# Cross-attention block with a routed mixture of experts: another order of the attention's last tiles, waits by bank, and a split of the tail's row sums

## What is computed

```python
x = x + xattn(layernorm(x), ctx, ctx, mask)   # 2 x 1024 rows of 256, 64 keys, 16 heads
x = x + ffn(layernorm(x))
# ffn, xf = the rows after the layer norm:
xa = xf @ P_w.T
C1, C2, C3 = (top3_softmax(xa @ U.T) for U in (U1, U2, U3))   # [rows, 12], three non-zeros a row
h = gelu(sum_e C1[:, e] * (xf @ W1[e].T))
y = sum_e C2[:, e] * (h @ W2[e].T) + C3 @ b2
```

## Time and profile before

| | |
|---|---|
| time, median of 3 runs (lowest to highest) | 380.97 us (378.94 to 382.95) |
| the profiled execution, its own time | 382.12 us |
| its span, first to last instruction | 380.4 us |
| busy, share of the span: PE, DVE, ACT, POOL | 86%, 67%, 52%, 62% |
| mean granted TensorE clock (1.00 is 2.4 GHz, 0.50 is 1.2 GHz) | 0.933 |

### The profile page before, as it was taken

The page is one execution under the profiler, slowest core; times in us unless marked ns, Lnnn a source line. Parts: engine busy times, 40 slices in busy tenths (PEclk is TensorE's granted clock), DMA queues, the critical chain, the costliest instruction groups (busy, mean ns, idle before and its releaser), DMA issues.

```text
span 380.4 us, 7721 instructions
## 1 busy us (share of the span) xinstructions
PE 326.9 (86%) x2071; PEld 287.2 (76%) x2071; DVE 253.9 (67%) x842; ACT 198.6 (52%) x485; POOL 236.5 (62%) x335
## 2 busy tenths in 40 slices
PE   4879989998987668598798979989998979999970
PEld 3569889987977657487788968868887979997850
DVE  3899878897877741646687825576759435553795
ACT  2477989995856604013666751333316756871000
POOL 4359578766875771100677776777724777776692
PEclk9999999998989965879899999989999998999995
DMA  7900111321311282300466736552244766740973
GB/s 221 370 14 4 57 55 57 116 83 57 99 61 44 90 294 70 106 0 15 130 190 206 246 126 223 187 186 105 103 150 130 224 195 188 216 154 1 332 271 117
DMA packets 33889, 52.21 MB, mean 137 GB/s; under 512 B 6090, under 2 KB 23860, under 8 KB 33720
## 3 DMA queue, kind: packets, MB, share of 16 engines
q1 hardware_dynamic: 26472, 35.35, 29.5%
q0 software_dynamic: 6816, 16.24, 11.9%
q10 hardware_dynamic: 560, 0.13, 0.2%
HBM read 29.75 MB, written 24.82 MB: 143 GB/s over the span
## 4 chain that ended last, share of the span: by engine, by line
PE 53%; DVE 15%; issue 10%; POOL 9%; ACT 6%; DMA 4%; DVEq 0%; SPq 0%; ACTq 0%; POOLq 0%
PE banks L1657 32%; PE banks L1940 3%; PE banks L1746 3%; PE banks L1728 3%; PE banks L1703 2%; POOL w_l L592 2%; POOL list_rows L720 2%; PE banks L1713 2%; PE banks L1716 2%; PE banks L1718 2%; DVE q_hl L1070 2%; DMA y_token<-prob,bo_sb 1%; DMA late_rows<-list_rows 1%; PE banks L1789 1%; DVE xn L1279 1%
## 5 line engine op out<-in xcount | busy, mean ns | idle before, releaser
L1657 PE MATMUL banks<-w_h,xd 128*128 128x512 f32 x288 | 96.2, 416 | 2.8 <-ACT prob L931 2.8
L1657 PE MATMUL banks<-w_h,bt 128*128 x328 | 71.0, 309 | 4.8 <-DVE bt L1442 4.8
L1657 PEld LDWEIGHTS banks<-w_h,xd 128*128 128x128 f32 x288 | 56.7, 200 | 16.5 <-issue 3.2
L1657 PE MATMUL banks<-w_l,xd 128*128 128x512 f32 x144 | 59.3, 412 | 0.0
L1657 PEld LDWEIGHTS banks<-w_h,bt 128*128 128x128 f32 x328 | 51.3, 194 | 7.6 <-issue 6.4
L694 POOL DMA_INDIRECT y_token<-prob,bo_sb x42 | 41.0, 975 | 23.4 <-DVE bo_sb L1444 13.3
L1657 PE MATMUL banks<-w_l,bt 128*128 x164 | 47.2, 288 | 0.0
L694 POOL DMA_INDIRECT y_token<-prob_t,bo_sb x40 | 39.6, 989 | 12.1 <-issue 6.0
L1279 DVE SCALAR_TENSOR_TENSOR xf_t<-banks,mask_all,xf_t 128x256 f32<-128x256 f32 x60 | 25.6, 479 | 24.0 <-ACT xf_t L841 12.2
L1442 DVE TENSOR_TENSOR bt<-banks,bt 128x256 fp32r<-128x256 f32 x82 | 33.9, 416 | 9.6 <-ACT bt L925 9.5
L925 ACT ACTIVATE bt<-banks 128x256 fp32r<-128x256 f32 x82 | 30.9, 381 | 15.3 <-PE banks L1940 14.7
(11 more groups left out here) (231 smaller groups left out, 762.7 us busy)
## 6 DMA issues: line engine op xcount, KB each, us to landing
late_rows<-list_rows SPq DMA_DIRECT2D x62, 136.0 KB, 2.8
stage<-in_w_t_dram SPq DMA_DIRECT2D x12, 512.0 KB, 3.7
list_rows<-wo_sb SPq DMA_DIRECT2D x26, 136.0 KB, 2.5
stage<-y_token SPq DMA_DIRECT2D x8, 384.0 KB
late_rows<-y_token SPq DMA_DIRECT2D x6, 384.0 KB, 3.8
mid<-y_token SPq DMA_DIRECT2D x6, 384.0 KB, 4.4
out_dram<-x_all SPq DMA_DIRECT2D x16, 128.0 KB, 2.0
wq_sb<-list_rows SPq DMA_DIRECT2D x10, 136.0 KB
```

The lines of the kernel that those rows point to most:

```text
L1657: ins = pe.matmul(dst, a(c), b(c), start=(i == 0), stop=(i == len(terms) - 1))
```

## The change

It reorders what the engines do in rounds 14 to 16 of the attention and just behind them, and it changes four waits or orders later on:

- PE: early pairs 0 and 1 ahead of the values of tile 14, pair 2 ahead of those of tile 15, pair 3 behind round 15's output projection, pair 4 ahead of that of round 16; tiles 13 and 14 are transposed in round 16 and behind it, ahead of pairs 8 to 11; only tile 15 is left for the block stage.
- ACT: `copy_xf` of tiles 11 and 12 first in its round; tiles 13 and 14 and weight chunk 11 ahead of the block stage.
- DVE: `xd_low` of tiles 11 and 12 right behind `a_low`; `stats2` ahead of the table's last part; in round 15 only one pair's sum stands ahead of the last `a_low`; chunk 11 ahead of the block stage.
- POOL: tiles 6 and 7 are sent a round later, behind `inverse_deviation2(13)`; `place_h(3)` stands behind the first of the layer-2 sends.
- Slots 2 and 9 wait for the block that last used the pair's own bank, no longer for all blocks. `transpose_h` stands after four pairs. The first block's low part of the second stage stands ahead of `last_sum(8)`.
- Tail: POOL makes both adds for tiles 0 to 7 and one for tiles 8 to 11; DVE makes the other one there.

```diff
# POOL
                 if t == 14:
                     send_x(5)
+                if t == 15:
                     send_x(6)
                     send_x(7)
...
-            place_h(HS - 1)
             for n in range(S):
+                if n == 1:
+                    place_h(HS - 1)
...
-                pool.wait_ge(y_rest, t + 1)
-                pool.tensor_tensor(quarter(y, 0), quarter(y, 0), quarter(y, 1), ALU.add).then_inc(y_whole, 1)
+                if t < POOL_TAILS:
+                    pool.wait_ge(y_rest, t + 1)
+                    pool.tensor_tensor(quarter(y, 0), quarter(y, 0), quarter(y, 1), ALU.add).then_inc(y_whole, 1)
# ACT, attention loop and behind it
+                if t in (14, 15):
+                    copy_xf(t - 3)
                 if t < T:
                     copy_pt(t)
-                if t == 14:
-                    copy_xf(11)
                 a_high(t - 1)
...
                 if t == 15:
-                    copy_xf(12)
                     copy_z(12)
                     first_pair(0)
                 if t == 16:
-                    first_pair(1)
+                    copy_xf(13)
...
-                if 2 <= t < 16:
+                if t >= 2:
                     normalise2(t - 2)
...
+            first_pair(1)
+            copy_xf(14)
+            normalise2(T - 1)
+            split_weights(CHUNKS - 1)
# DVE, attention loop and behind it
-                a_low(t - 1)
+                if t < T:
+                    a_low(t - 1)
+                if t in (14, 15):
+                    xd_low(t - 3)
...
-                if t == 14:
-                    table_places(0)
-                    early_spread(2)
...
                 stats2(t - 1)
                 if t == 14:
-                    xd_low(11)
+                    table_places(0)
+                    early_spread(2)
                     split_low(EARLY)
                 if t == 15:
-                    xd_low(12)
-                    sum_pairs(0, range(1, 4))
+                    sum_pairs(0, range(1, 2))
+                    a_low(T - 1)
+                    sum_pairs(0, range(2, 3))
+                if t == 16:
+                    sum_pairs(0, range(3, PAIRS))
                     split_low(EARLY + 1)
-                if t == 16:
-                    sum_pairs(0, range(4, PAIRS))
+                    xd_low(13)
                     split_low(EARLY + 2)
-            sum_pairs(1, range(1, PAIRS))
+            sum_pairs(1, range(1, 3))
+            xd_low(14)
+            split_low(CHUNKS - 1)
+            sum_pairs(1, range(3, PAIRS))
# DVE, tail
             def sum_tail(t):
-                dve.wait_ge(y_whole, t + 1)
                 y = tail_in[t % TAIL_LOADS]
+                if t < POOL_TAILS:
+                    dve.wait_ge(y_whole, t + 1)
+                else:
+                    dve.wait_ge(y_rest, t + 1)
+                    dve.tensor_tensor(quarter(y, 0), quarter(y, 0), quarter(y, 1), ALU.add).then_inc(y_pair, 1)
+                    dve.wait_ge(y_pair, S1 + t - POOL_TAILS + 1)
# PE, attention loop and behind it
                 if t == 14:
                     logits(10)
                     logits(11)
+                    early_pairs(0, 1)
                 if t == 15:
                     logits(12)
+                    early_pairs(2, 3)
...
-                if t == 15:
-                    early_pairs(1, 3)
+                if t == 14:
+                    early_pairs(1, 2)
                 if t < T:
                     weigh_values(t, t // TPB)
-                if t == 14:
-                    early_pairs(0, 1)
+                if t == 16:
+                    early_pairs(4, 5)
                 output_project(t - 1)
                 if t == 15:
                     early_pairs(3, 4)
-                if t == 16:
-                    early_pairs(4, 6)
...
-                if 13 <= t < 15:
-                    transpose_xf(t - 2)
-            early_pairs(6, 8)
+                if t in (13, 14, 16):
+                    transpose_xf(min(t - 2, 13))
+            early_pairs(5, 8)
+            transpose_xf(14)
# PE, slots 2 and 9
                     if slot in (EARLY_SLOTS, MID):
-                        pe.wait_ge(block_out, FIRST[1 if slot < MID else 2])
+                        done = FIRST[1 if slot < MID else 2]
+                        if bank < HT:
+                            pe.wait_ge(block_lo, max(g for g in range(done) if g % HT == bank) + 1)
+                        else:
+                            pe.wait_ge(block_out, max(g for g in range(done) if Y_BANK[g % HT] == bank) + 1)
```

More of the change, by code:

```diff
@@ L62, in xattn_ffn_kernel @@
     BATCH_REGS = 24
+    POOL_TAILS = 8
     TABLE = 15
@@ L1621, in _ @@
             h_low(15)
-            sum_pairs(8, range(3, PAIRS))
+            for pair in range(3, PAIRS):
+                sum_pair(8, pair)
+            block_low(FIRST[1])
+            last_sum(8)
             for j in range(BLOCKS[1]):
-                block_low(FIRST[1] + j)
+                if j > 0:
+                    block_low(FIRST[1] + j)
                 if j < 7:
```

35 lines of the change are left out of this document (17 added, 18 removed).

## The result

The changed kernel takes 371.46 us (median of four runs, 370.42 to 372.05) against 381.84 of the kernel before in the same runs (378.94 to 382.95): a ratio of 0.974, 95% interval 0.967 to 0.980. It is faster by 10.4 us; 17.0 were forecast. The profiled execution took 371.75 us, its span is 369.9, its mean granted clock 0.947.

The account below looks back on a forecast made before the run. PE's waits and lower clock in the attention's end, then GpSimd's sends, were taken as bounds. The second block stage 18.2 us earlier, less 1.2 in the tail, gave 17.0 off: 364.0 us against the median, range 357.6 to 371.5.

Parts of the forecast that it names:

- the term for the lower clock: Attention's end: PE loses 3.0 us to the lower clock level, against 9.5 before, from one stretch of some 6 us.
- the rest of that sum: Attention's end: 29.8 us of PE work at the upper level plus 7.0 us of remaining waits.
- GpSimd's shift behind the first block product: First block stage: GpSimd gains 5.1 us by starting with the first copy, less 1.0 for slowly arriving blocks.
- place_h: List sends: moving place_h(3) behind the first sends gains 1.3 us of the 2.4 it cost.
- First block stage and dense stage: PE gains 2.0 us in the first block stage, then 2.19 and 1.81 us from two dense-stage waits that go.
- the 1.81 that was to go: Dense stage: with four pairs ahead of transpose_h, PE's wait of 1.81 us there goes.
- Tail: Kernel's end: four adds moved from GpSimd to VectorE cost 1.2 us more, with bounds of 0.3 and 3.8.
- clock as before: Rival, attention's end: PE still loses 9.5 us to the lower level, 6.5 more than assumed; 370.5 us, chance 0.12.
- GpSimd hides it: Rival, block sends: GpSimd's first send still trails the first copy by 5.1 us; 367.2 us, chance 0.08.
- Alternation of pairs and sums: Rival, attention's end: each of pairs 3 to 11 waits for its sums, costing 10 us; 374.0 us, chance 0.05.
- the lower level throughout: Rival, attention's end: PE stays at the lower level all through, a loss of 9.8 us; 390.8 us, chance 0.03.
- One of the prediction's signs of being wrong: List sends: the forecast is wrong if GpSimd starts on time and list sends still end after 268.

Follow-up runs that it names:

- e4: The changed kernel with the tail as before (GpSimd adds all rows of all twelve tiles): 366.61 us, ratio 0.954 to the kernel before.
- e6: The changed kernel run again on another chip, nothing edited: 369.98 us, ratio 0.970 to the kernel before.
- e7: The changed kernel with place_h(3) back ahead of the first list send: 369.44 us, ratio 0.969 to the kernel before.
- e11: e10 with 32 unneeded matmuls in five places where PE waits: 357.51 us, ratio 0.932 to the kernel before.
- e8: The changed kernel with only the attention's end reordered; later waits, transpose_h, low part, place_h and tail as before: 370.87 us, ratio 0.975 to the kernel before.
- e9: The changed kernel with twelve unneeded matmuls ahead of the values of tile 15: 365.54 us, ratio 0.953 to the kernel before.
- e12: The changed kernel with unneeded matmuls in four places ahead of the transpose of tile 11 only: 364.08 us, ratio 0.950 to the kernel before.
- e2: The changed kernel with PE loading the block stage's registers ahead of the transpose of tile 14: 365.48 us, ratio 0.948 to the kernel before.
- e1: The changed kernel with weight chunk 8's subtraction behind the copy of the table's rows: 367.08 us, ratio 0.958 to the kernel before.
- e10: e3 with the tail as before (POOL_TAILS = 12): 362.52 us, ratio 0.945 to the kernel before.
- e3: The changed kernel with the edits of both e1 and e2: 362.36 us, ratio 0.943 to the kernel before.

## Why the prediction was too low

The move was right in sign and in kind; three fifths of its size came (10.4 of 17.0 us). Step by step:

- **The step that failed is the term for the lower clock**, "to the lower clock I give 3.0 us, against 9.5 before: one stretch of some 6 us of work". The profiled execution had 13.8 us at the lower level there and an end of 43.1 us instead of 39.8. With 3.1 us at the lower level (e4, e6, e7) the same order takes 38.7, so the rest of that sum holds: 38.7 - 3.1 / 2 = 37.1 at the upper level, where 29.8 + 7.0 = 36.8 were forecast. Two errors offset each other in it: PE stands 6.0 us (38.70 - 32.69 in e6), not 7.0, and its work at the upper level is about 31 us (31.45 in e11 with the four added matmuls), not 29.8. The prediction took 82% busy for the whole of the 23.5 us, and that was the share of ten of them. The waits were found where they were forecast, at 1.86 for 1.7 and 1.99 for 2.6; that each of them may be followed by the lower level, and so cost half of the 6.9 or 3.4 us that it lasts (0.57 over 8 us, 0.58 over 4), was priced once and not per wait.
- **The same term was left out ahead of tile 11.** The forecast took the 126.32 us of one trace as fixed. With 7.6 us at the lower level that execution was a lucky one: the eleven later traces without fillings there lie between 127.3 and 131.1, with 10.2 to 18.4 us at it. This is the other 3.4 us. Over several traces it weighs more than the first: in the five that have the new order just as it is (changed, e4, e6, e7, e8) the lower level lasts 7.4 us on average in the end, where about 6 were forecast, and 13.5 ahead of it, where 7.6 were taken over.
- Were these two a mere accident of one profile, the median would not show them. It does: the eight runs of the changed kernel have mean clocks of 0.942 to 0.953 and lie at 367.73 to 372.05, all above the forecast's 364.0. The forecast had priced the luckier end of what the level does. How much of the gain is missing differs with the chip all the same: e4, the same order with the old tail, for which 18.2 us would have been forecast, gained 17.1 (366.61 against 383.69).
- GpSimd's shift behind the first block product: forecast 5.1 - 1.0 = 4.1, measured 6.61 - 2.29 = 4.3 at the first send and 3.9 at the last. Right.
- place_h: 1.3 forecast, nothing to be seen in e7, about 0.9 over all traces. Behind it a wait of 2.17 us for the first list rows' landing came up, which the forecast did not name.
- First block stage and dense stage: of the two waits of the earlier trace rows the 2.19 us went, and the 1.81 that was to go stayed at 1.68; that step of the prediction failed. PE finished 7.1 us earlier all the same, relative to the first block product (6.0 forecast), mainly because it took 37.8 us from the first to the last block product, where it had taken 41.8: 4.0 less, 2.0 forecast. In the kernel before 3.5 us of that stage were at the lower level (0.96 over 44.27 us), now none are, which the forecast did not count. The lists gained 4.1 (5.4 forecast), so the lists and not PE now set the start. That 103.12 came for 103.2 is luck: the errors cancel.
- Tail: 1.1 for 1.2. Right, and with the cause that was given: the new adds run alone and take 0.42. It was close, for GpSimd ends at 358.91 and the first of them starts at 359.04.
- Rivals: "clock as before" gave 370.5, and the time agrees best with it, though not as it was put: in the attention's end the lower level fell from 23.5 us to 13.8 in one trace and 3.1 in others; what stayed high was the total with the stretches ahead of it. "GpSimd hides it" is half true (lists ahead of PE) without costing what it gave. Alternation of pairs and sums and the lower level throughout were not seen. One of the prediction's signs of being wrong did appear, GpSimd on time and list sends that end after 268 (the last starts at 269.63); what it showed was the late first block product, from which the last list send is 96.8 us away, where 95.5 were forecast (261.6 - 166.1).

The prediction doubted the rule of the Trainium skill, "TensorE: Matmul & The Clock Gate", section "What's actually happening", that the throttled state is the default and activity releases it. In e9, e11 and e12 added activity alone removed the lower level where it was put, so the traces agree with the rule; the forecast that would have followed from it, 3.0 us lower still, would have been further off, since the waits that were left sufficed to bring the level back. Why ten microseconds at 82% busy stayed at 0.50 in the kernel before no run here tells.

## What to carry to other kernels

Read the clock of one trace as one draw: ask for each wait on TensorE of a microsecond or more what it costs if the lower level follows, and compare the mean clock of several runs before taking a stretch's length as fixed. Where such a wait can't be removed, a few matmuls into a free bank, shorter than the wait and ahead of it in the queue, are worth a try: here 32 of them gained 5.0 us. Set kernels side by side on one chip: here the ratio of the same order differed by more than 1% between chips. When an edit moves the start of a long chain on another engine (here 35 block and 36 list sends), follow that chain from its own first instruction, and look for the wait that takes the place of the one removed.

## What the runs showed of the hardware

- What follows the same wait in the same program differs from one execution to another. Behind 1.86 us ahead of the values of tile 15 the lower level came in all seven traces that have this wait, but for 6.9 us in the changed kernel and for 3.1 in e6: the values took 3.38 us (changed, e12), 3.31 (e2) and 3.29 (e8) in some, 2.38 in others (e4, e6, e7). Behind 1.47 to 1.54 us pair 8 ran at the lower level in the changed kernel, e1, e8 and e12 and at the upper in e4, e6, e7 and e9. The Trainium skill, "TensorE: Matmul & The Clock Gate", section "What's actually happening", says that the number of slow matmuls at a kernel's start varies from run to run; here the same is seen in its middle.
- The lower level followed waits of 1.0 to 1.9 us here. With five of them cut to 0.5 us or below (e11: 0.40, 0.34, 0.45, 0.32 and 0.25 us are left) none of it is left between 32 us and the end of the dense stage; e10, without the matmuls, had 3.6 us of it in the attention's end alone. A shorter wait is not safe either: in e3 and e10 it came where 0.72 us had preceded the values. In e1 the same 0.72 us was not followed by it.
- 10.7 us more at the lower level cost 4.4 us in the attention's end (changed against e7), less than half of it, since PE also stands there.
